# The last block's feed-forward in two token halves with paired channels, in a fused cross-attention and feed-forward kernel

## The reference, cut to what matters

```python
# first part: x = x + attention(layernorm(x), ctx)
q = layernorm_per_head((layernorm(x) @ Wq)) * gq + bq
k = layernorm_per_head((ctx @ Wk)) * gk + bk ; v = ctx @ Wv
x = x + (softmax(q @ k.T / sqrt(32)) @ v) @ Wo
# second part: x = x + ffn(layernorm(x))
s = z @ Win + bin_                       # (tokens, 64), z = layernorm(x)
h = relu(s[..., None] * W1 + b1)         # (tokens, 64, 16)
g = einsum('btmh,mh->btm', h, W2) + b2   # (tokens, 64)
x = x + g @ Wout + bout
```

## Time and profile before

| | us |
|---|---|
| median of 3 runs | 468.31 |
| lowest and highest | 466.9, 468.89 |
| profiled execution, its own time | 467.24 |
| its span | 465.4 |

### The profile page before, as it was taken

How to read it: one execution, slowest core, us unless ns; L and a number is a source line. 1 busy time by engine, 2 the same in 40 slices (tenths; PEclk the granted TensorE clock), 3 DMA queues, 4 the chain that set the end, 5 groups by cost and what they waited for, 6 DMA issues and landing times.

```text
span 465.4 us, 7733 instructions
## 1 busy us (share of the span) xinstructions
PE 430.0 (92%) x2328; PEld 281.7 (61%) x2328; DVE 329.5 (71%) x646; ACT 326.2 (70%) x623; POOL 247.7 (53%) x330
## 2 busy tenths in 40 slices
PE   4899999999999999999999999999969988999933
PEld 2565877385677648673868467765744563367712
DVE  4886886576469966798479956875788445654986
ACT  2869759978659973998399965985397619863650
POOL 4549987266454654567454735545463405154970
PEclk9999999999999999999999999999997999699976
DMA  8454994853932284519541683039500781070004
GB/s 293 151 181 105 211 226 106 191 142 68 223 90 71 63 241 111 120 44 228 156 113 51 169 215 70 4 78 250 115 15 1 218 201 38 23 249 2 1 1 180
DMA packets 25289, 58.34 MB, mean 125 GB/s; under 512 B 5920, under 2 KB 6432, under 8 KB 22176
## 3 DMA queue, kind: packets, MB, share of 16 engines
q1 hardware_dynamic: 24992, 57.58, 47.4%
q10 hardware_dynamic: 256, 0.26, 0.2%
HBM read 22.18 MB, written 8.39 MB: 66 GB/s over the span
## 4 chain that ended last, share of the span: by engine, by line
PE 76%; DVE 5%; ACT 5%; issue 4%; SPq 4%; DMA 2%; POOL 1%; POOLq 0%; DVEq 0%; ACTq 0%
PE bank L1988 34%; PE bank L2084 11%; PE bank L1994 8%; PE bank L2072 7%; PE bank L2051 6%; PE bank L2152 3%; PE bank L2087 3%; DVE bank L922 2%; PE bank L2137 2%; PE bank L2096 2%; ACT hid L1502 1%; DMA q_stack<-mxt 1%; ACT prob L1420 1%; PE bank L2059 1%; DMA xin<-in_x_dram 1%
## 5 line engine op out<-in xcount | busy, mean ns | idle before, releaser
L838 DVE TENSOR_REDUCE mx<-bank 128x4 f32<-128x512 f32 x128 | 84.4, 684 | 43.7 <-PE bank L2051 43.7
L1420 ACT ACTIVATE prob<-bank 128x512 f32<-128x512 f32 x128 | 72.4, 596 | 39.9 <-PE bank L2072 35.8
L2084 PE MATMUL bank<-prob,v_kv 128*32 128x512 f32 x256 | 68.1, 630 | 0.6 <-ACT prob L1420 0.3
L2087 PE MATMUL bank<-prob,den_sel 128*32 128x512 f32 x256 | 67.7, 630 | 0.0
L568 POOL TENSOR_TENSOR qt_lo<-u,qt_hi 128x512 fp32r<-128x512 f32 x32 | 41.3, 1292 | 47.4 <-ACT u L1397 47.3
L1502 ACT ACTIVATE hid<-s_in,b_col,w_col 128x256 f32<-128x256 f32 x118 | 63.0, 597 | 1.8 <-DVE s_in L891 1.4
L922 DVE SCALAR_TENSOR_TENSOR bank<-hid,w_col,bank 128x256 f32<-128x256 f32 x120 | 57.9, 483 | 7.9 <-ACT hid L1502 0.9
L1988 PE MATMUL bank<-wq_hi,zt_hi 128*128 128x512 f32 x128 | 53.3, 417 | 2.4 <-DVE zt_lo L825 2.4
L2072 PE MATMUL bank<-q_stack,k_stack 97*128 97x512 f32 x128 | 49.8, 448 | 3.9 <-DMA q_stack<-mxt 1.7
L1988 PE MATMUL bank<-wq_lo,zt_hi 128*128 128x512 f32 x128 | 50.5, 395 | 0.0
L1988 PE MATMUL bank<-wq_hi,zt_lo 128*128 128x512 f32 x128 | 50.5, 394 | 0.0
(11 more groups left out here) (171 smaller groups left out, 902.1 us busy)
## 6 DMA issues: line engine op xcount, KB each, us to landing
q_stack<-qt_hi SPq DMA_DIRECT2D x64, 256.0 KB, 4.5
xin<-in_x_dram SPq DMA_DIRECT2D x36, 256.0 KB, 3.8
q_stack<-qt_lo SPq DMA_DIRECT2D x32, 256.0 KB, 4.4
x<-in_x_dram SPq DMA_DIRECT2D x28, 256.0 KB, 4.3
out_dram<-x SPq DMA_DIRECT2D x28, 256.0 KB, 2.3
att<-in_L_xattn_Wk_dram SPq DMA_DIRECT2D x1, 1024.0 KB, 6.5
x<-in_L_xattn_Wq_dram SPq DMA_DIRECT2D x4, 256.0 KB, 7.1
hid<-in_L_xattn_Wv_dram SPq DMA_DIRECT2D x1, 1024.0 KB, 9.6
```

What stands on the lines that cost most here:

```text
L838: dve.tensor_reduce(mx[:, j, :].rearrange("p (g i) -> p i g", g=G)[:, 2 * half + r, :], maxs_banks[T][half][j][r][:, :].rearrange("p (g n) ...
L1420: act.activation(prob[:, h % PR, :], score_bank[t][h][:, :], ACT.Exp, scale=SCALE).then_inc(exp_done, 1)
L2084: pe.matmul(at_bank[t][c][rows(n), :], v_kv[kv_of(t)][:, n * HD:(n + 1) * HD], prob[:, n % PR, :], start=True, stop=True)
L2087: ins = pe.matmul(den_bank[t][rows(n + 2), :], den_sel[:, c, :], prob[:, n % PR, :], start=c == 0, stop=c == C - 1)
```

## The change

Three things.

1. **The last block's feed-forward in two token halves.** Tiles 0 and 1 are half 0, tiles 2 and 3 half 1. Statistics, the deviation's factor, s, its scaling, the split of the sum: each is done for a half by itself (`aggregate_half`, `guess_half`, `newton_half`, `spread_rstd_half`, `move_rstd_half`, `project_s_half`, `scale_half`, `g_high_half`, `g_low_half`), in PSUM banks of the half's own.
2. **Pairs of channels' units in the row halves.** In a half, rows 0 to 63 and rows 64 to 127 both hold s of the same 256 tokens. One unit works on hidden unit 2n in the upper rows and 2n + 1 in the lower rows, so a half has 8 units and the block still 16, each 128 x 256. `pair_tables` (DVE) builds the weights for it once, in 14 small instructions. The last matmul, `project_y_last(j)`, contracts over all 128 rows, which adds both parts, and yields tile j alone: the tiles of half 0 come first. Four of the 16 units run on GpSimd instead of five.
3. **New orders.** All five lists, in prologue, iteration and epilogue, are in a new order, with new bank tables and new bare waits on TensorE. Among it: `stack_keys(0)` goes behind the twelve `stack_q(0, *)` transfers and `load_x(3, 2)`; `selectors` goes from the head of DVE's list to the end of its prologue; in the epilogue `max_scores(6, 1, 2)`, `max_scores(6, 1, 3)` and `turn_max(6)` go ahead of the end of `project_o(4, *)`, and `scores(7, 0)` behind `project_s(5)`; `spread_rstd(6)` goes ahead of `project_s(6)`.

The diff, cut:

```diff
+SHARED_FROM = BLOCKS - 2
+LAST = BLOCKS - 1
+HP = HH // 2
+LAST_UNITS = (2, 5, HP + 2, HP + 5)
...
+        def units_shared(t):
+
+            return LAST_UNITS if last(t) else POOL_UNITS if shared(t) else ()
...
+        def in_half(a, half):
+
+            return a[:, HT * P * half:HT * P * (half + 1)]
...
+        def place(T, j):
+
+            return j if last(T) else 2 * (j % HT) + j // HT
...
             def prologue():
...
+                load_x(2, 0)
+                load_x(2, 1)
                 load_wo()
-                load_x(2, 0)
-                stack_keys(0)
-                load_x(2, 1)
-                load_wout()
                 load_x(2, 2)
                 load_x(2, 3)
+                load_wout()
                 stack_q(0, 0)
...
                 load_x(3, 2)
+                stack_keys(0)
+                load_x(3, 3)
                 stack_keys(1)
-                load_x(3, 3)
...
+            def aggregate_half(half):
+                dve.wait_ge(ln2_step, LAST * 5)
+                dve.wait_ge(bn2_done, LAST * TB + HT * half + HT)
+                dve.tensor_copy((spare_last if half else spare)[:, :], bn2[:, 0, 0:1])
+                for j in range(HT * half, HT * (half + 1)):
+                    dve.bn_aggr(mv2[:, j, :], bn2[:, j, :]).then_inc(tail_mv[half], 1)
+
+            def newton_half(half):
+                dve.wait_ge(rstd_spread, LAST)
+                own = slice(HT * half, HT * (half + 1))
+                newton(ln2[:, :, own], mv2[:, own, 1], 1, tail_act[half], 2, tail_step[half], 0)
+
+            def scale_half(half):
+                dve.wait_ge(tail_s_mm[half], 1)
+                dve.wait_ge(tail_moved[half], 1)
+                dve.tensor_tensor(in_half(s_in, half), of_half(tail_s_bank[half]), in_half(s_in, half),
+                                  ALU.mult).then_inc(tail_s[half], 1)
...
+            def pair_tables():
+
+                dve.wait_ge(bias_folded, 5)
+                for half in range(2):
+                    rows = slice(M * half, M * (half + 1))
+                    for dst, src in ((pair_w1, w1_col), (pair_b1, b1_col), (pair_nb1, nb1_col), (pair_w2, w2_col),
+                                     (pair_wb, wb_col)):
+                        dve.tensor_scalar(dst[rows, :], src[rows, half::2], 1.0, None, ALU.mult).then_inc(pairs_done, 1)
...
             def add_hidden(T, hh):
 
-                if shared(T) and hh in POOL_UNITS:
+                if hh in units_shared(T):
                     dve.wait_ge(hid_shared, pool_units(T, hh) + 1)
                 else:
                     dve.wait_ge(hid_done, act_units(T, hh) + 1)
...
+                if last(T):
+                    n, total = hh % HP, of_half(tail_s_bank[hh // HP])
+                    weight, bias = pair_w2[:, n:n + 1], pair_b2
...
+            def project_s_half(half):
+
+                pe.wait_ge(z2t_done, LAST * TB + HT * half + HT)
+                for c in range(C):
+                    for rows in (slice(0, M), slice(M, 2 * M)):
+                        ins = pe.matmul(of_half(tail_s_bank[half][rows, :]), win[:, c, :],
+                                        in_half(z2t_of(LAST)[:, c, :], half), start=c == 0, stop=c == C - 1)
+                ins.then_inc(tail_s_mm[half], 1)
+
+            def project_y_last(j):
+
+                pe.wait_ge(tail_g[j // HT], 1)
+                cols = slice(j * P, (j + 1) * P)
+                g_hi, g_lo = at_hi_of(LAST)[:, 0, cols], at_lo_of(LAST)[:, 0, cols]
+                for n, (g, w) in enumerate(((g_hi, wout_hi), (g_hi, wout_lo), (g_lo, wout_hi))):
+                    ins = pe.matmul(y_bank[LAST][j][:, :], g, w[:, :], start=n == 0, stop=n == 2)
+                ins.then_inc(tail_y, 1)
```

The tail of DVE's new list, from the end of block 6's sum on:

```diff
+                add_hidden(6, 14)
+                scale_half(0)
                 add_hidden(6, 15)
+                aggregate_half(1)
                 add_hidden(7, 0)
+                g_low(6)
                 add_hidden(7, 1)
                 add_hidden(7, 2)
+                newton_half(1)
                 add_hidden(7, 3)
                 add_hidden(7, 4)
                 add_hidden(7, 5)
+                scale_half(1)
...
+                residual2(7, 0)
+                g_low_half(1)
+                residual2(7, 1)
+                residual2(7, 2)
                 residual2(7, 3)
```

1484 lines of the change are left out of this document (773 added, 711 removed).

## The result

| | before | after |
|---|---|---|
| median of 11 runs, us | 467.33 | 464.64 |
| lowest and highest | 465.67, 471.09 | 462.76, 465.9 |
| profiled execution, own time | 467.24 | 465.12 |
| its span | 465.4 | 463.3 |

The ratio after to before is 0.9923, interval 0.9897 to 0.995: 0.8% faster. I had put 467.9, no change that can be measured, with 464.0 to 471.2 as the range. The time is in the range, the verdict is not mine: of the three cases I gave "faster" 0.30.

What follows compares the result with a forecast made beforehand. TensorE was taken to bound the steady part, ScalarE the first drain stage, VectorE the tail. Fill +1.4, drain -0.8, tail -1.0 gave -0.4: span 465.0, median 467.9 us, range 464.0 to 471.2.

Steps and rivals of the forecast that it cites:

- the three cases: Whole kernel: no measurable change (within 0.5%) 0.47, faster 0.30, slower 0.18 and 0.05.
- an edit that only reorders calls there gives nothing as long as TensorE never waits: Steady part: TensorE is busy 50.00 of 50 us, so the new order there was priced at 0.
- the queue has caught up by then; I take nothing more: Fill, SyncE's queue: `stack_q(1, 0)` starts 3.9 later, but nothing is lost beyond the 1.4 at `scores(0, 0)`.
- my lower bound: Fill: 0, the keys land in time because TensorE is late for other reasons.
- My upper bound: Fill: 3.5 lost, where SyncE's queue stays late and 2.1 of the 3.9 reach TensorE.
- the key transfers at the fill's end: Slower rival: SyncE's queue stays late, fill loses 3.5, second drain stage brings nothing; median 470.8, chance 0.18.
- ScalarE's list is the limit: First drain stage: about 20.5 us of ScalarE work sets `project_o(5, 0, 0)`; gain 2.0 after 0.8 for the dip.
- The second stage: Second drain stage: `scores(7, 0)`'s wait is hidden, but block 7's exponentials begin relatively later; of 2.0 gained, 0.8 is left.
- The tail: VectorE's tail with block 7 in halves: the end comes 1.0 earlier, bounds 2.2 earlier and 1.2 later.
- the lock: Tail: small VectorE steps wait for GpSimd operations on a shared port pair; 0.5 at `newton_half(0)`, 1.1 at `newton_half(1)`.
- slower by the lock: Rival, tail: three small steps in each half meet a GpSimd operation, 6.6 instead of 1.6; median 472.9, chance 0.05.
- The faster rival: Drain stages give gains in full, 4.2, tail gains 1.0, fill loses 1.0; median 464.1, chance 0.30.

Runs made afterwards that it cites:

- steady_clean: Kernel before with the changed order of the steady part alone, and bank 4 instead of 0 for `scores(0, 8)`: 464.36 us, ratio 0.9922.
- keys_moved_alone: Changed kernel with before's fill and two edits against small waits, then SyncE's key stacks placed as in the change: 464.66 us, ratio 0.9932 to before.
- changed_shifted_back: Changed kernel with one unused one-column tensor, which moves its buffers 32 bytes further on: 464.92 us, ratio 0.9947 to before.

## Why the prediction came out as it did

**The step that failed: "an edit that only reorders calls there gives nothing as long as TensorE never waits".** I priced the steady part, 199 of 465 us, at 0, on a busy time of 50.00 of 50.00. TensorE's busy time is made of matmul durations of 0.4 and more whose starts lie 0.23 apart, so a wait of up to a few tenths disappears in it. Start to start, before had about 0.4 of such hidden wait in each block at one place, and eight changes of form more than the new order, worth 0.6. The changed order alone, steady_clean, measured -3.5 by the medians (interval of the ratio 0.9891 to 0.9953, so -2.2 to -5.1 of 468); its trace shows 2.1 of it at po 4. Without this step the forecast would have been a gain of 2.5 to 4, and not "no change".

**The second, in the fill: "the queue has caught up by then; I take nothing more".** The predicted +1.4 was for `scores(0, 0)`. The queue had not caught up: keys_moved_alone has it 3.4 of 4.4 us late still at the last `stack_q(1, *)`, so `q_high(2, 0)` and `spread(0, 0)` went late behind it. In the changed kernel this is a wait of 1.72 at `spread(0, 0)`, and the 1.4 at `scores(0, 0)` is 0.22. And the rest of the fill's new order, in the other four lists and in SyncE's loads, which I priced at nothing, costs 2.4 to 2.6 ahead of `scores(0, 0)`; my lower bound said that TensorE could be late for other reasons, but not that this would cost anything. The whole fill measured +2.7 (out of the changed kernel, by the ratios; 3.6 by the medians) and +3.6 (into the kernel before; 4.1 by the medians); the keys' place alone +4.5 to +4.9 in keys_moved_alone, with a dip of 1.7 that it brings there. My upper bound was 3.5. The mechanism and its place are those of the rival "the key transfers at the fill's end"; its sign `q_high(2, 0)` "over 4 later than 97.00" came true with 6.45 (4.37 of lateness TensorE already had at `scores(0, 0)`, which the rival did not foresee), its other, `scores(0, 0)` waiting over 3, did not. Its time, 470.8, didn't come about, because the steady part and the drain gave back more than it had them give.

**A term that was missing: the addresses.** The seven small tensors had no price in my sum. They measured -2.3 in the kernel before (interval 0.9926 to 0.9974) and -1.1 in the changed one, the second within its noise.

**The drain's first stage: right mechanism, size off by 0.8 to 1.** "ScalarE's list is the limit" holds: from `hidden(4, 0)` to po 5 I worked out 23.06, and it is 23.21 (344.06 to 367.27), with ScalarE busy 21.77 of 23.40. What I took off again for the dip, 0.8, was not to be taken off: the mean clock in the stage is 0.93 instead of 0.87, the stage is no longer with one dip in it than with none (44.44 and 44.68), and the gain over all traces is 3.0 instead of 2.0. `scores(6, 0)` came at 346.32, where I had 343 and had not foreseen its wait of 1.93 for VectorE's maxima; ScalarE's work covered it.

**The second stage: right.** 1.2 given back, 1.3 measured. But the reason was half right: `scores(7, 0)` still waits 1.64 for the row of maxima, and I had that wait hidden.

**The tail: right in the sum, -1.0 against -1.2, partly by luck.** It is the sum of three terms. `scale_s(6)` comes 0.42 earlier behind po 6 than before, where I had 0.84. From there to the last add it is 26.55 (429.53 to 456.08) for 26.45, so +0.1 where I had +0.8. From the last add to the last residual it is 4.70 for 5.59, -0.9 where I had -1.0. The middle term is the lock, overpriced: `newton_half(1)` took 0.9 instead of 1.9. The Trainium skill ("SBUF — State Buffer", "Who interferes with whom") has a VectorE operation with two SBUF inputs blocked until a GpSimd operation that reads SBUF, and started first, has finished. The traces agree for one kind of GpSimd operation and not for the other. In all 19 traces, each of the 29 small steps that begin during a GpSimd addition (`add_bout`, L619 after) ends 0.01 to 0.02 us behind it: the 1.13 of before, and after the 0.36 at 438.38, which ends with the addition of 437.43 to 438.72. But none of the 30 steps that begin during a GpSimd relu (L606, 445.75 to 446.99 after) waits for its end: the 20 among them with two SBUF inputs take 0.16 to 0.20, once 0.49. But for its first 0.14, `newton_half(1)` stood beside a relu. I had counted all GpSimd work alike, and the rival "slower by the lock" with me; it did not occur.

**The sum.** Steady -3.5, drain -1.7, tail -1.2, addresses -1.1 to -2.3, fill +2.7 to +4.1: -3.4 to -6.0. Measured: -2.7 by the medians, -3.6 by the ratio (interval -2.3 to -4.8). The parts give more than the whole. Some are counted twice: the drain's 1.7 holds 0.3 that is the addresses', and the steady part's 3.5 is 2.1 to 2.3 by the traces. Each carries an interval of 1 to 2 us; they add up within these, not better. The faster rival, 464.1, had the number almost right (464.64) for a reason that is only partly so: its 4.2 from the drain are 1.7, and the rest came from where it looked for nothing.

**What beats both kernels.** old_fill_mended, the changed kernel with before's order of the whole fill on all five engines and a bank of its own for `scores(0, 8)`, has 459.76, a ratio of 0.9836 (0.9801 to 0.9871): twice the gain of the change as it was made.

**Open.** Which call of the fill's new order costs the 2.4 ahead of `scores(0, 0)`; what the changed kernel would take with the keys alone put back; why the addresses matter, and which tensor's; and whether the two parts of the steady gain, which were told apart by place only, can be had one without the other.

## What to carry to other kernels

Where an in-order engine is "100% busy", measure start to start against the spacing of the same instruction in an undisturbed stretch before an edit there is priced at nothing. A batch of transfers moved back in a queue can cost more at its last follower than at its first (here 2.0 and a clock dip against 0.9): follow every transfer behind it until the queue has an idle gap, and price the wait there. Then look whether the engine that waits is late for a reason of its own, as it was here. If an edit allocates anything, run the old kernel with the same unused allocation beside it, or the edit is credited with what an address does.

## What the runs showed of the hardware

- The spacing of 128 x 512 matmuls depends on where their operands are allocated: 0.229 us at one place, 0.233 32 bytes further on or 224 bytes before it, at the same order and clock. In the kernel before it is worth 0.5% of the whole (interval 0.3% to 0.7%). No run says which operand.
- Changes of form cost TensorE time that no bracket shows: a stretch of 512-column matmuls between transposes takes 0.08 to 0.11 us more than its count times the spacing, one between two groups of 32-column matmuls 0.20, in a block of the kernel before.
- A start of TensorE can be 0.3 us late without a bracket in its timeline and without less busy time (264.40 in the kernel before). That it is a wait was argued from VectorE's times, not shown.
- A small VectorE step with SBUF inputs that begins during a GpSimd addition of two SBUF tensors ends with it (29 of 29, 0.01 to 0.02 us behind); during a GpSimd relu of about the same length (1.2 us) it does not wait for the end (30 of 30).
- A stretch of lower clock need not show in the time: where ScalarE's list is the limit, in the drain's first stage, one dip of 3.4 us leaves 44.44 (after), none 44.68 (changed_shifted_back). Two separate ones make it 45.64 to 45.96. In the fill, where TensorE sets the pace, a dip of 3.4 us costs 1.6 to 1.7.
